# Attention and routed feed-forward on one core: where the gate scales are applied, and how one tile's work is shared between VectorE and GpSimd

## The reference

```python
Q_, K_, V_ = Qr @ Wq + bq, Kr @ Wk + bk, Vr @ Wv + bv            # 16 heads of 8 numbers -> 64
scores = einsum('blhk,blgk->blhg', Q_, K_) / sqrt(64)
attn = softmax(scores, axis=-1)                                  # over the 16 keys g of a token
x = x + (einsum('blhg,blgv->blhv', attn, V_).reshape(B, L, 16 * 64) @ Wo + bo)
h = layernorm(x)
probs = softmax(h @ router_w); gate, index = top_k(probs, 2)
# for each token and each of its two experts e:
v = h @ (wv[e] * sv[e]);  y = gelu(h @ (w[e] * s[e]))            # 128 -> 512
out = (v * y) @ (w1[e] * s1[e])                                  # 512 -> 128
x = x + sum of gate * out over the two experts
```

## Time and profile before

| | |
|---|---|
| median of 3 runs | 273.85 us |
| profiled execution | 273.13 us, span 271.4 us |
| TensorE matmul busy | 227.8 us (84%) |
| VectorE busy | 185.7 us (68%) |
| GpSimd busy | 147.4 us (54%) |
| ScalarE busy | 118.8 us (44%) |
| attention steps 2 to 13 | 32.5 to 114.4 us of the span |
| first feed-forward products | 128.8 us |
| last feed-forward products | 254 us |

### The profile page before, as it was taken

The page is one execution under the profiler, slowest core; times in us unless marked ns, Lnnn a source line. Parts: engine busy times, 40 slices in busy tenths (PEclk is TensorE's granted clock), DMA queues, the critical chain, the costliest instruction groups (busy, mean ns, idle before and its releaser), DMA issues.

```text
span 271.4 us, 6278 instructions
## 1 busy us (share of the span) xinstructions
PE 227.8 (84%) x1820; PEld 217.5 (80%) x1821; DVE 185.7 (68%) x494; ACT 118.8 (44%) x297; POOL 147.4 (54%) x162
## 2 busy tenths in 40 slices
PE   7897999993999749946989879897999999999700
PEld 7787988992999649936978869797999999999700
DVE  3799799999799996985527586744545555555326
ACT  2443535852365403453236475445554555555100
POOL 6956789975798848730046545555334442433400
PEclk9997999999599968997599999999999999999975
DMA  4979999994000100012101121113222212000058
GB/s 142 303 152 439 369 333 386 380 379 167 4 20 29 33 20 22 10 40 59 23 20 39 52 70 41 39 43 81 58 62 60 52 45 56 19 19 19 8 192 272
DMA packets 25659, 30.93 MB, mean 114 GB/s; under 512 B 2795, under 2 KB 17038, under 8 KB 25504
## 3 DMA queue, kind: packets, MB, share of 16 engines
q1 hardware_dynamic: 21708, 25.28, 28.6%
q0 software_dynamic: 2528, 4.77, 5.6%
q10 hardware_dynamic: 1396, 0.55, 0.8%
HBM read 16.26 MB, written 14.79 MB: 114 GB/s over the span
## 4 chain that ended last, share of the span: by engine, by line
PE 45%; DVE 24%; issue 16%; DMA 6%; POOL 3%; SPq 2%; ACT 2%; DVEq 0%; POOLq 0%; ACTq 0%
PE bank L995 18%; PE bank L1014 8%; DVE qk L1143 7%; PE bank L918 6%; PE bank L881 6%; DVE pv L325 4%; DMA routed<-rows,pos 3%; PE bank L812 2%; DMA pv<-expert_out 2%; POOL routed L557 2%; DVE counted L1255 2%; DVE neg_max L1175 1%; DVE shifted L1179 1%; DVE rowsum L1193 1%; SPq L396 1%
## 5 line engine op out<-in xcount | busy, mean ns | idle before, releaser
L569 POOL DMA_INDIRECT expert_out<-yo,xs x39 | 38.3, 982 | 52.2 <-DVE yo L1365 30.9
L557 POOL DMA_INDIRECT routed<-rows,pos x32 | 33.0, 1031 | 37.0 <-ACT rows L685 20.5
L995 PE MATMUL bank<-xsT,g_tile 128*128 128x128 f32 x312 | 43.0, 282 | 5.3 <-ACT xsT L742 2.8
L881 PE MATMUL bank<-ident,qk 128*128 128x128 f32 x256 | 35.8, 301 | 11.7 <-DVE qk L1143 11.7
L325 POOL TENSOR_TENSOR pv<-probs,ctx_sb 128x1408 f32<-128x1408 f32 x14 | 40.1, 2862 | 8.2 <-DVE probs L1197 6.0
L995 PEld LDWEIGHTS bank<-xsT,g_tile 128*128 128x128 f32 x312 | 38.7, 195 | 6.7 <-issue 6.5
L881 PEld LDWEIGHTS bank<-ident,qk 128*128 128x128 f32 x256 | 32.7, 157 | 13.1 <-issue 12.9
L995 PE MATMUL bank<-xsT,v_tile 128*128 128x128 f32 x312 | 42.1, 279 | 0.0
L1014 PE MATMUL bank<-w_sb,hid 128*128 x312 | 41.6, 276 | 0.4 <-DVE yo L1365 0.3
L1356 DVE TENSOR_TENSOR hid<-bank,act_sb 128x512 f32<-128x512 f32 x39 | 26.9, 688 | 19.4 <-PE bank L995 14.1
L995 PEld LDWEIGHTS bank<-xsT,v_tile 128*128 128x128 f32 x312 | 38.8, 196 | 0.0
(11 more groups left out here) (167 smaller groups left out, 312.4 us busy)
## 6 DMA issues: line engine op xcount, KB each, us to landing
routed<-pad_rows SPq DMA_DIRECT2D x4, 2080.0 KB, 20.2
xs<-routed SPq DMA_DIRECT2D x39, 65.0 KB
g_sb<-in_L_ffn_w_dram SPq DMA_DIRECT2D x1, 2048.0 KB, 10.4
g_scale<-in_L_ffn_s_dram SPq DMA_DIRECT2D x1, 2048.0 KB, 14.8
v_sb<-in_L_ffn_wv_dram SPq DMA_DIRECT2D x1, 2048.0 KB, 25.2
pv<-expert_out SPq DMA_DIRECT2D x3, 512.0 KB, 4.8
x_sb<-in_x_dram SPq DMA_DIRECT2D x4, 256.0 KB, 6.0
ctx_sb<-in_ctx_dram SPq DMA_DIRECT2D x4, 256.0 KB, 6.7
```

Of the source, the lines that this page charges most:

```text
L557: pool.indirect_dma_start(out=routed[:, :], out_offset=bass.IndirectOffsetOnAxis(ap=pos[:, m % TOP, m // TOP:m // TOP + 1], axis=0), in_=r ...
L569: pool.indirect_dma_start(out=expert_out[:, :], out_offset=bass.IndirectOffsetOnAxis(ap=xs_i[:, t % XB, P:P + 1], axis=0), in_=yo[:, t % X ...
L881: mm = nc.tensor.matmul(part, qk[:, b, i, c * P:(c + 1) * P], ident[:, :], start=(i == 0), stop=(i == HD - 1), is_transpose=True)
L995: mm = nc.tensor.matmul(psum[:, n * P:n * P + P], weights[:, c % 2, n * P:n * P + P], xsT[:, c % 2, :], start=True, stop=True)
```

## The change

The gate scales leave GpSimd. VectorE now multiplies the 512 gate columns of a tile with their scales on the way into `g_tile` (L1350 of the new kernel), and ScalarE copies the value weights. GpSimd's share of the 16 keys depends on the tile: 11 for tiles 0 to 4 and 8, all 16 for tiles 5, 6 and 7, 9 for tiles 9 to 13. VectorE's `positions` moves from the end of steps 6 and 10 to behind `qk` in steps 7 and 11; the scatters are spread anew, and two of group 1 stand behind the last step. The copy of the counts becomes a sum over an axis of length one.

```diff
         def pool_keys(t):
-            return {NT - 2: LAST_KEYS, NT - 1: 0}.get(t, POOL_KEYS)
+            return {NT - 2: LAST_KEYS, NT - 1: 0}.get(t, H if 5 <= t < 8 else 9 if t >= 9 else POOL_KEYS)
+        def pool_shares(t):
+            return sum(pool_keys(u) > 0 for u in range(t + 1))
+        def dve_shares(t):
+            return sum(pool_keys(u) < H for u in range(t + 1))
+        EARLY_SENT = 6
         def sends(n):
-            return {9: 2, 10: 5, 11: G * TOP} if n < EARLY_G - 1 else {8: 2, 9: 5, 10: G * TOP}
+            return {9: 1, 10: 3, 11: 6, 12: G * TOP} if n < EARLY_G - 1 else {9: 1, 10: 3, 11: 6}
...
-        HF = F // 2
-        GATES_SCALED = {2: (0, 1), 3: (2, 3, 4), 4: (5, 6, 7), 6: (8, 9), 7: (10, 11, 12), 8: (13, 14, 15)}
...
-                    for c in GATES_SCALED.get(AHEAD + G * g + j, ()):
...
-                        if c != GATES_SCALED[AHEAD + G * g + j][0]:
-                            pool.wait_ge(pv_dve, AHEAD + G * g + j)
-                        pool.tensor_tensor(g_sb[:, cols], g_sb[:, cols], g_scale[:, cols], ALU.mult).then_inc(g_scaled, 1)
...
                 for t in STEADY:
                     step(t // G, t % G)
+                scatters(EARLY_G - 1, EARLY_SENT, G * TOP)
                 scatters(NG - 2, 0, 4)
...
-                    nc.scalar.copy(g_tile[:, c % 2, :], g_sb[:, bass.ds(at, F)]).then_inc(g_tile_ready, 1)
+                    nc.scalar.copy(v_tile[:, c % 2, :], v_sb[:, bass.ds(at, F)]).then_inc(v_tile_ready, 1)
...
+                    if a := group_at(g, j, PLACES + 1):
+                        positions(a[0])
                     if a := tile_at(g, j, 1):
...
                         normalise(a[0])
-                    if a := group_at(g, j, PLACES):
-                        positions(a[0])
...
                 def value_share(t):
+                    if pool_keys(t) == H:
+                        return
...
-                    v.tensor_copy(carry, prefix[:, G, :]).then_inc(carry_ready, 1)
+                    v.tensor_reduce(carry, prefix[:, G, :].unsqueeze(2), AX_X, ALU.add).then_inc(carry_ready, 1)
...
-                    v.tensor_copy(v_tile[:, c % 2, :], v_sb[:, bass.ds(at, F)]).then_inc(v_tile_ready, 1)
+                    v.tensor_tensor(g_tile[:, c % 2, :], g_sb[:, bass.ds(at, F)], g_scale[:, bass.ds(at, F)],
+                                    ALU.mult).then_inc(g_tile_ready, 1)
```

More of the change, by code:

```diff
@@ L517, in step @@
                     a = tile_at(g, j, 1)
-                    if a and a[0] < NT - 2:
+                    if a and pool_keys(a[0]):
                         t, b = a
@@ L525, in step @@
                         values(pool, t, b, 0, pool_keys(t)).then_inc(pv_pool, 1)
-                    for c in GATES_SCALED.get(AHEAD + G * g + j, ()):
[L528 to L531, removed]
-                        if c != GATES_SCALED[AHEAD + G * g + j][0]:
-                            pool.wait_ge(pv_dve, AHEAD + G * g + j)
-                        pool.tensor_tensor(g_sb[:, cols], g_sb[:, cols], g_scale[:, cols], ALU.mult).then_inc(g_scaled, 1)
                     if (g, j) == divmod(NT - AHEAD - 2, G):
                         second_rstd(NG - 2)
-                    for lag in range(PLACES, PLACES + G):
+                    for lag in range(PLACES, PLACES + G + 1):
                         if a := group_at(g, j, lag):
@@ L753, in ffn @@
                     if a := ffn_tile(i, k, 2, (2,)):
-                        gate_weights(*a[:2])
+                        value_weights(*a[:2])
                         rows_turned(*a[:2])
@@ L762, in _ @@
                 normed(NG - 2)
-                gate_weights(0, 0)
+                value_weights(0, 0)
                 exponentials(NT - 1)
@@ L770, in _ @@
                 rows_turned(0, 0)
-                gate_weights(1, 1)
+                value_weights(1, 1)
                 rows_but_gates(NG - 2)
@@ L777, in _ @@
                 residual(NT - 1)
-                gate_weights(2, 2)
+                value_weights(2, 2)
                 rows_turned(2, 2)
                 gelu(1, 1)
-                gate_weights(3, 3)
+                value_weights(3, 3)
                 rows_turned(3, 3)
                 gelu(2, 2)
-                gate_weights(4, 4)
+                value_weights(4, 4)
                 rows_turned(4, 4)
@@ L787, in _ @@
                 gelu(3, 3)
-                gate_weights(5, 5)
+                value_weights(5, 5)
                 turned(NG - 1)
@@ L792, in _ @@
                 rows_but_gates(NG - 1)
-                gate_weights(6, 6)
+                value_weights(6, 6)
                 rows_turned(6, 6)
@@ L911, in value_sum @@
                         pe.wait_ge(sv_ready, 1)
-                    pe.wait_ge(pv_dve, t + 1)
-                    if t < NT - 2:
-                        pe.wait_ge(pv_pool, t + 1)
+                    pe.wait_ge(pv_dve, dve_shares(t))
+                    if pool_keys(t):
+                        pe.wait_ge(pv_pool, pool_shares(t))
                     if first_on(t):
@@ L1339, in _, with gate_weights @@
                 mid, late = slice(EARLY, MID), slice(MID, TILES)
-                def value_weights(t, c):
+                def gate_weights(t, c):
                     if isinstance(t, int) and t == 0:
-                        dve.wait_ge(ld_wv, 16)
+                        dve.wait_ge(ld_wg, 16)
+                        dve.wait_ge(ld_gs, 16)
                     at = dve.value_load(w_off[0:1, bass.ds(t, 1)], min_val=0, max_val=(E - 1) * F)
@@ L1369, in ffn @@
                     if a := ffn_tile(i, k, 2, (2,)):
-                        value_weights(*a[:2])
+                        gate_weights(*a[:2])
                     if a := ffn_tile(i, k, 1, (1,)):
@@ L1377, in _ @@
                     step(t // G, t % G)
-                value_weights(0, 0)
+                gate_weights(0, 0)
                 maximum(NT - 1)
@@ L1384, in _ @@
                 value_share(NT - 1)
-                value_weights(1, 1)
+                gate_weights(1, 1)
                 positions(NG - 2)
@@ L1389, in _ @@
                 second_statistics(NT - 1)
-                value_weights(2, 2)
+                gate_weights(2, 2)
                 hidden(1, 1)
                 gated(0, 0)
-                value_weights(3, 3)
+                gate_weights(3, 3)
                 left_table(EARLY)
@@ L1396, in _ @@
                 gated(1, 1)
-                value_weights(4, 4)
+                gate_weights(4, 4)
                 tiles_left(1)
@@ L1401, in _ @@
                 gated(2, 2)
-                value_weights(5, 5)
+                gate_weights(5, 5)
                 rows_left(mid, MID - EARLY, mid_ready)
@@ L1405, in _ @@
                 gated(3, 3)
-                value_weights(6, 6)
+                gate_weights(6, 6)
                 choices(NG - 1)
```

10 lines of the change are left out of this document (5 added, 5 removed).

## The result

| | before | changed |
|---|---|---|
| median | 274.17 us (4 runs, 273.4 to 275.05) | 266.76 us (4 runs, 264.94 to 267.26) |
| ratio | | 0.9717, interval 0.9661 to 0.9772 |
| profiled execution | 273.13 us, span 271.4 | 266.83 us, span 265.1 |

The kernel is 7.4 us faster, inside the forecast range of 258 to 267, but 5.4 us short of the forecast itself. I cut both profiles at three marks: the start of `qk` of step 2, the end of the attention steps (VectorE's first operation on the early table), and the first feed-forward products. The column "forecast" is the 12.4 us of the prediction, each term put into the stretch where its rows lie (one of the three held normalisations stands ahead of step 2).

A forecast was written before the change was run, and what follows sets the result against it. VectorE was taken to pace the attention steps, TensorE close behind, and TensorE the feed-forward stage. Attention terms sum to -13.1 us, -12.4 with part 6: 260.7 us profiled, 261.4 median; own bounds 258 to 264, range to 267.

The forecast's parts named there:

- signs named: Counts near 0.15 us, TensorE gaps under 1.6 at clock 1.00, steps 2 to 13 in 69, first products near 115.5.
- Part 1: Attention steps: without GpSimd's gate products, three held normalisations give 0.50 us each, -1.5 us.
- Part 2: Steps with `positions`: counts by a sum, `positions` behind `qk`; either removes the stall, counted once, 2.3 us twice, -4.6 us.
- Part 3: TensorE's 4.65 us gap shrinks to 1.3, clock kept; steps 8 and 12 fall to 5.2 us, -5.0 us.
- the first rival: TensorE's clock falls all the same in step 7 or 11, costing 1.3 to 2.4 us each: 263 to 266 us; chance 0.20.
- Part 4: Step 10: with 9 keys and two scatters on average, GpSimd no longer holds VectorE's value share, -1.6 us.
- Part 5: Key split: tiles 5 to 7 save VectorE 1.75 us, tiles 9 to 13 cost 1.35, together -0.4 us.
- The rival of a late GpSimd: GpSimd's 16 keys hold VectorE 0.5 to 1 us in three or four steps, or part 7 shows: 263 us; chance 0.10.
- The warning sentence: Skill's rule giving elementwise work to VectorE; by it the sum would lose the 1.75 us of tiles 5 to 7.
- Part 6: Feed-forward: VectorE's gate product takes 0.69 us against a copy's 0.43, counting at four places, +0.7 us.
- the slower rival: GpSimd's indirect transfers hold the feed-forward gate product up to 1.66 us: 288 us; chance 0.04, shared with other slow slips.
- Part 7: Tail: group 1's last scatter issued some 4.3 us later, the load just fits: 0, at most +1.5 us.

The follow-up runs named there:

- e4: Kernel before with gate scales in VectorE's copy, value weights copied by ScalarE, no gate products on GpSimd; routing and keys as before: 273.76 us, ratio 1.0012.
- e1: Kernel before with one edit, the eight counts carried by a sum instead of a copy: 267.94 us, ratio 0.9822.
- e2: Kernel before with `positions` moved behind `qk` and the changed kernel's scatters; counts still by the copy: 264.29 us, ratio 0.9707.
- e8: Kernel before with counts by a sum, `positions` behind `qk`, and scatters spread 2, 3, 3; gate scales and keys as before: 268.35 us, ratio 0.9805.
- e7: Changed kernel with the scatters of both early groups spread 2, 3, 3 behind `positions`, none behind the last step: 268.27 us, ratio 0.9785.
- e3: Kernel before with counts by a sum, `positions` behind `qk` and the changed kernel's scatters; gate scales and keys as before: 264.87 us, ratio 0.9709.
- e5: Changed kernel with the key split undone, GpSimd taking 11 keys of every tile up to 13: 265.55 us, ratio 0.9684.
- e6: Changed kernel with VectorE's gate product replaced by a plain copy, the gate scales left out of the computation: 264.08 us, ratio 0.9654.
- e9: Changed kernel with extra TensorE identity products, 20 ahead of the value sums of tile 14 and 16 before the first turned rows: 263.54 us, ratio 0.9638.
- e10: Changed kernel with 4 extra TensorE identity products behind each turned tile 0 to 3, at the start: 264.75 us, ratio 0.9678.
- e11: Kernel before with counts by a sum, later `positions`, fillers in tail and start, and the last rows' table one feed-forward tile later: 262.23 us, ratio 0.9620.
- e12: Whole changed kernel with fillers in tail and start, and the last rows' table one feed-forward tile later: 262.38 us, ratio 0.9613.

## Why the prediction was right, and where it was not

Right in direction, and in the range by some luck. The forecast's own bounds ended at 264 us; the range went on to 267 only for the rival in which TensorE's clock falls in the steps. That did not happen, and the 266.76 us came about by other losses. Of the miss 1.3 us is in the steps and 4.8 outside them (both profiles; the forecast for the profiled execution was 260.7, it took 266.83). Of the signs named, the counts, TensorE's gaps and its clock in the steps came true. The first products came at 120.97 us instead of 115.5.

**Part 1, held normalisations: right.** Steps 3 and 5 fell by 0.49 and 0.80 us, 0.30 of the latter by the keys of tile 5, and e4 shows the holds gone by the gate move alone. The third lay ahead of step 2 and can't be seen behind the start's own difference.

**Part 2, counts: right, and "counted once" too.** e1 and e2 each remove the stall of 2.3 us.

**Part 3, TensorE's gap: right.** Steps 8 and 12 fell by 4.70 us; forecast were 5.0, less 0.27 for two keys. The gap was smaller than the 1.3 us forecast in step 7 and about that in step 11, and the clock held. e1, with 2.39 us, lost it. So the first rival did not come true here. But the length of the gap alone does not decide it: in e8 TensorE waited 2.35 us in step 9, and its matmuls ran on at full rate (TensorE):

```profile
81.06 1.97 PE L918 MATMUL bank<-ident,pv 128*128 128x128 f32 x16 [2.35 <-DVE pv L325]
```

**Part 4, the held share: right.** Steps 10 and 11 together fell by 3.36 us; the terms (2.3 for the counts, 1.6 for the share, less 0.54 for keys) make 3.4. e7 and e8 bring the hold back with three scatters in a step. The reason, GpSimd's time per step, is confirmed. e4 shows what the term rests on: with the scatters of before the share still takes 1.87 us in step 9 and 2.43 in step 10, without any gate product. e3 shows the other half: with the scatters spread but the gate products in place it takes 1.98 and 1.18. With both edits and 11 keys (e5) it is 1.16 and 1.20. So the spread of the scatters frees the share in step 10, and in step 9 it takes the spread and the gate move together. The lighter share of 9 keys ends only the last 0.4 us of the hold.

**Part 5, keys: mis-sized, and the whole miss of the steps.** Steps 6 and 7 fell by 2.54 us, where the sum had 3.9; the others, steps 10 and 11 taken together, came within 0.2 of it. By e5, tiles 5 to 7 gave 0.6 us instead of 1.75. Tiles 9 to 13 cost 0.6 instead of 1.35, because 11 keys bring part of the hold back. The first error is the one that shows: I counted VectorE's saved 0.8 us in steps 6 and 7 in full, but in step 6 VectorE came ahead of TensorE and waited 0.69 us for its scores. Steps 5 and 6 together took 12.99 us with 16 keys and 13.03 with 11; only step 7 gained, 0.57. The rival of a late GpSimd came once, with 0.27 us on one normalisation. The warning sentence, that the Trainium skill gives elementwise work to VectorE ("GPSIMD Engine Reference", Engine selection), weighed the right term: by that rule the sum lost 1.75 us, and the runs took 1.15 of them.

**Part 6, gate product in the feed-forward stage: mis-sized, and not fully explained.** It takes 694 ns and is not held, so the slower rival is refuted: 718 ns was the longest of 39. But it cost about 2 us instead of 0.7. The largest wait for it, 1.35 us at 168.63, is not the reason: it stands behind the operations of the last table on VectorE's queue, and so did the copy. In the same tile TensorE waited 1.16 us for the copy in e6, and 1.15 us in the kernel before, at 174.99. Against e6 the changed kernel loses 1.0 us from the first tile's products to the second's, where both run at half clock for a time, and 1.8 us over the next ten tiles. It wins 1.1 over the three behind them and loses 0.7 over the ten after that, which the sum took as free. Which of this is the product's own, and which is the clock's, one profile of each can't tell.

**Part 7, late scatters: the step that failed.** The term was "0, at most +1.5 us", and the tail took 1.8 us more. Forecast was a last scatter 4.3 us later that "just fits". It came 7.1 us later (9.9 against 2.8 behind the steps), for two reasons. Four more scatters are four times 1.28 us, 5.1, and I had taken more off for GpSimd's shorter product than there was. And one issue took 2.69 us, 1.7 more than usual, while VectorE worked through its 16-key product (109.79 to 112.07), with the two around it 0.5 us longer together. The tail's +1.8 us divides on ScalarE: its queue was free 0.86 us later, counted from the end of the steps (the value sums at half clock throughout), and then it waited 0.93 us for the rows. The experiments show why one remedy is not enough: e7 brings the rows early and meets the half clock, e9 mends the clock and meets the late rows. The profile before had early rows, and half clock for a shorter time: its value sums took 3.49 us, but the router products behind them ran at 1.00 again. Its 14.35 us is the shortest tail of all fourteen profiles, and not to be had for sure: e1 and e4, with its scatters, took 15.9 and 16.2 us, without late rows. So in the changed kernel the late rows are enough for the tail of 16.2 us, but half clock alone gives much the same. Early scatters with a filled tail were not run. As an estimate from e9's wait of 1.76 us they would win that much, and lose 2.2 in the steps if made as in e7.

**Ahead of step 2: not in the sum.** The instructions up to there are the same in the changed kernel, e5, e6, e7 and e9, yet step 2 began at 34.23, 34.01, 31.10, 32.79 and 33.86 us. It goes with TensorE's clock: never low in e6 (31.10), 0.50 from about 22 to 25 us in before (32.48), 0.50 from about 14 to 20 in the changed kernel (34.23). Which of them an execution gets looks like chance. It is not excluded that the gate move makes the late start likelier: of the kernels without filled start, four of the six that have the move began later than 33.8 us, and none of the five that don't. Filling the waits removed the low stretches in e10, e11 and e12 (32.57, 32.54, 32.25), at some cost, since e6 was earlier still. The forecast should have had 1.5 us either way for it.

So of the change, the later `positions` with its spread scatters is what pays. On top of them the sum, the keys and the gate move add nothing that these runs can tell.

## What to carry to other kernels

Price each stretch of the kernel apart, the ones that nobody touched too: the two that I had priced at -0.5 and 0 gave back 3.5 us. How much of that an edit caused is a second question: kernels that are the same in a stretch differed by 3 us in it here. When two chains meet (here rows by transfer and ScalarE's queue), ask how far behind the second one is before moving the first; an edit that mends one alone shows nothing. An instruction moved out of a queue's busy place can be worth more than one made faster: `positions` one step later saved both its hold and TensorE's clock, while the cheaper operation saved only the hold. It needs the transfers that hang on it spread as well: without that (e8) the median was 268.35 us, no better than the cheaper operation alone (267.94).

## What the runs showed of the hardware

- **An indirect issue on GpSimd is stretched by VectorE's product with two SBUF operands.** 0.97 us alone, 1.80 to 1.89 us beside a product of 1.07 us, and 2.69 us beside one of 2.28 (3.01 in e8). In these cases the product was running when the issue began, and the extra time is about what was left of it: 1.72 us of 1.84 in the changed kernel, 2.04 of 2.17 in e8. An issue that began 0.41 us ahead of a product of 1.07 us kept its 0.97 (91.33 in the changed kernel). I had looked for the opposite hold, of VectorE by the issue, and the product did not show it. The Trainium skill, "GPSIMD Engine Reference", section Key points, says that both engines share SBUF interfaces and contend on instructions with two SBUF inputs; the trace agrees, and shows that it works in this direction too.
- **The copy is held to the end of GpSimd's product, and form decides.** A copy of eight elements took 2.49 us beside it, a reduction of the same eight 0.15, and the copy 0.30 where the product was nearly over.
- **TensorE's clock** stayed at 1.00 behind waits of 1.2 us (two in step 11 of the changed kernel) and 1.34 (e2), fell behind 2.39 (e1), 2.86 and 4.65. Length alone does not decide: it stayed at 1.00 behind 2.35 (step 9 of e8) and 2.45 (144.94 in e12), and fell behind 2.48 (147.13 in e10). In the start it fell behind 1.19 (before, 22.50) and stayed behind 1.20 (e6, 22.48), in the same place of the stream. Idle-time products kept it at 1.00 wherever they were put.
